# Last layer of a four-layer model: the two softplus functions with positive part and absolute value on ScalarE

## The reference, cut to what matters

```
dt = jax.nn.softplus(jnp.einsum('blr,dr->bld', time_step, dt_proj_w) + dt_proj_b)
delta = jax.nn.softplus(dt + dt_proj_b)
...
state = jnp.exp(d_t[..., None] * A) * state + (d_t * u_t)[..., None] * b_t[:, None, :]
```

## Time and profile before

| | |
|---|---|
| timed, median of 3 | 3816.14 us |
| profiled execution, its own time | 3796.93 us |
| span of the profiled execution | 3794.5 us |
| mean granted TensorE clock | 0.814 |
| TensorE matmul busy | 2954.5 us (78%) |
| VectorE busy | 2671.8 us (70%) |
| ScalarE busy | 1789.3 us (47%) |
| GpSimd busy | 448.2 us (12%) |

### The profile page before, as it was taken

One profiled execution on the slowest core, in us unless ns is written; L12 is line 12 of the kernel. 1 busy time (PEld: TensorE's weight loads), 2 busy tenths in 40 slices (PEclk: granted clock), 3 DMA queues, 4 the chain that ended last, 5 costly groups with the idle time before them and its releaser, 6 DMA issues. The chain is left out here.

```text
span 3794.5 us, 60184 instructions
## 1 busy us (share of the span) xinstructions
PE 2954.5 (78%) x19822; PEld 2399.8 (63%) x19822; DVE 2671.8 (70%) x7020; ACT 1789.3 (47%) x4073; POOL 448.2 (12%) x339
## 2 busy tenths in 40 slices
PE   3888888888989989899555567777777777777777
PEld 2666767767878878788444545555555555555555
DVE  3554554556666666666676279888888888888888
ACT  1222222225555555555334345555555555555555
POOL 0000000000000000000111312222211222222222
PEclk9887787788999999999667767677777777777777
DMA  5000000000000000000200211111111111111112
GB/s 163 0 0 0 0 0 0 0 0 1 0 0 0 0 0 0 0 0 0 65 8 15 58 53 46 46 45 35 45 46 45 46 45 46 45 45 41 40 45 67
DMA packets 66485, 103.57 MB, mean 27 GB/s; under 512 B 16808, under 2 KB 42032, under 8 KB 66352
## 3 DMA queue, kind: packets, MB, share of 16 engines
q1 hardware_dynamic: 63104, 97.36, 7.8%
q0 software_dynamic: 2048, 4.20, 0.4%
q10 hardware_dynamic: 1200, 0.27, 0.0%
HBM read 92.59 MB, written 9.21 MB: 27 GB/s over the span
## 5 line engine op out<-in xcount | busy, mean ns | idle before, releaser
L966 ACT ACTIVATE b_neg<-b_neg,b_nmax 128x128 f32<-128x128 f32 (+1 forms) x512 | 228.5, 447 | 272.9 <-DVE b_nmax L1074 271.6
L2229 POOL TENSOR_TENSOR d_state<-d_state 128x1024 f32<-128x1024 f32 x96 | 239.4, 2515 | 677.3 <-DVEq L2430 677.3
L2157 ACT ACTIVATE d_probs<-l_bank,w_b 128x256 f32<-128x256 f32 x512 | 210.8, 469 | 225.1 <-PE l_bank L2005 222.7
L2016 PE MATMUL l_bank<-w_w,d_probs 128*128 128x128 f32 x2048 | 267.7, 287 | 49.0 <-DVE same_head L2436 49.0
L2016 PEld LDWEIGHTS l_bank<-w_w,d_probs 128*128 128x128 f32 x2048 | 258.3, 201 | 64.5 <-issue 53.2
L2418 DVE TENSOR_TENSOR_SCAN d_state<-w,d_state 128x1024 f32<-128x1024 f32 x128 | 289.2, 2280 | 6.2 <-issue 6.2
L2005 PE MATMUL l_bank<-xnT,w_w 128*128 128x256 f32 x1024 | 248.1, 386 | 13.1 <-ACT d_probs L2157 13.1
L1062 DVE SCALAR_TENSOR_TENSOR b_gated<-b_th,l_bank 128x256 f32<-128x256 f32 x256 | 107.6, 420 | 207.9 <-ACT b_th L960 203.6
L607 ACT ACTIVATE a_hT<-l_bank,lnb,lnw 128x128 f32<-128x128 f32 x128 | 46.5, 468 | 423.9 <-PE l_bank L553 423.9
L518 PE MATMUL l_bank<-a_vmem,a_memT 128*128 128x128 f32 x768 | 185.2, 364 | 71.4 <-ACT a_h L602 71.4
L96 POOL TENSOR_TENSOR ln_rstd<-ln_var_eps,minus_half 128x2 f32<-128x2 f32 x51 | 35.3, 692 | 1670.5 <-DVE ln_var_eps L90 1670.5
(11 more groups left out here) (406 smaller groups left out, 7651.1 us busy)
## 6 DMA issues: line engine op xcount, KB each, us to landing
d_bct<-l_bc SPq DMA_DIRECT2D x132, 512.0 KB, 4.1
x_sorted<-x SPq DMA_DIRECT2D x1, 2176.0 KB, 15.2
w<-in_L_ffn_w_dram SPq DMA_DIRECT2D x1, 2048.0 KB, 10.1
w_w<-in_L_ffn_W_dram SPq DMA_DIRECT2D x1, 2048.0 KB
c2e_xg<-x_sorted SPq DMA_DIRECT2D x16, 128.0 KB, 2.3
y_sorted<-c2e_yo SPq DMA_DIRECT2D x16, 128.0 KB, 1.8
out_dram<-x SPq DMA_DIRECT2D x1, 2048.0 KB, 8.7
gating<-n_kernel_gating_EDF_dram SPq DMA_DIRECT2D x1, 1024.0 KB, 6.5
```

Of the source, the lines that this page charges most:

```text
L966: done = nc.scalar.activation(neg[:, h % RP, cols], neg[:, h % RP, cols], ACT.Exp, bias=nmax[:, h % RP, a:a + 1], scale=-1.0, accum_out=to ...
L2016: done = nc.tensor.matmul(bank[:, 4 + e % 2, a * D:(a + 1) * D], hid[:, e % 2, k, a * P:(a + 1) * P], w.w2[:, e, k, :], start=(k == 0), st ...
L2157: done = v.activation(hid[:, e % 2, k, :], bank[:, b, i * T:(i + 1) * T], ACT.Gelu, bias=w.b1[:, e, k:k + 1])
L2229: nc.gpsimd.tensor_tensor(st[i][:, 0:SG, :], st[i][:, 0:SG, :], st[i][:, SG * g:SG * (g + 1), :], ALU.add)
```

## The change

The argument work of both softplus functions moves from VectorE to ScalarE, and the second sum and `du` move from the end of a sequence to between the maxima of the second and the third score block of the next. `dneg_ready` is replaced by `half_ready`, which the first sum raises. `softplus_arg`, `first_part`, `second_part` and `third_part` go.

```
             def log_part(m, j):
-                act.wait_ge(dneg_ready, 2 * m + j + 1)
-                v.activation(dneg[:, :, :], dneg[:, :, :], ACT.Exp)
+                if j == 0:
+                    act.wait_ge(dt_in_psum, m + 1)
+                    act.wait_ge(rot_ready, m + 1)
+                    src = bank[:, 3, :].rearrange("p (i t) -> p i t", i=CI)
+                else:
+                    act.wait_ge(half_ready, m + 1)
+                    src = delta
+                for i in range(CI):
+                    v.activation(dv[:, i, :], src[:, i, :], ACT.Relu, bias=w.dt_b[:, i:i + 1])
+                for i in range(CI):
+                    done = v.activation(dneg[:, i, :], src[:, i, :], ACT.Abs, bias=w.dt_b[:, i:i + 1])
+                if j == 0:
+                    done.then_inc(dt_taken, 1)
+                v.drain()
+                v.activation(dneg[:, :, :], dneg[:, :, :], ACT.Exp, scale=-1.0)
                 v.drain()
                 v.activation(dneg[:, :, :], dneg[:, :, :], ACT.Ln, bias=1.0).then_inc(dlog_ready, 1)
...
             def softplus_sum(m, j):
                 dve.wait_ge(dlog_ready, 2 * m + j + 1)
-                done = v.scalar_tensor_tensor(out=delta[:, :, :], in0=dv[:, :, :], scalar=0.0, in1=dneg[:, :, :],
-                                              op0=ALU.max, op1=ALU.add)
-                if j == 1:
-                    done.then_inc(delta_ready, 1)
+                v.tensor_tensor(delta[:, :, :], dv[:, :, :], dneg[:, :, :], ALU.add)\
+                    .then_inc((half_ready, delta_ready)[j], 1)
+
+            def state_drive(m, par):
+                softplus_sum(m, 1)
                 v.drain()
                 v.tensor_tensor(du[:, :, :], delta[:, :, :], xs[:, par, :, :], ALU.mult)
...
-            first_part(0)
-            second_part(0)
-            third_part(0, 0)
+            softplus_sum(0, 0)
...
                         heads_max(blk)
                         if blk == 0:
                             norm_stats(nc, c, s, n + 1)
+                        if blk == 1:
+                            state_drive(n, par)
                     norm_rows(n + 1, 1 - par)
+                    v.drain()
...
                     add_expert(4)
-                    first_part(n + 1)
                     add_expert(5)
...
                     inner_stats()
-                    second_part(n + 1)
+                    softplus_sum(n + 1, 0)
                     inner_apply(rows[:, :, :], w.g2, w.be2, 2 * n + 2).then_inc(gate_ready, 1)
-                    third_part(n + 1, 1 - par)
```

More of the change, by code:

```diff
@@ L1853, in layer3 @@
         dt_taken = sem("dt_taken")
-        dneg_ready = sem("dneg_ready")
+        half_ready = sem("half_ready")
         dlog_ready = sem("dlog_ready")
```

## The result

Timed: 3872.5 us, the median of 4 runs (3866.2 to 3874.1), against 3814.0 us for the kernel before (4 runs). The ratio is 1.015, with a 95% interval of 1.0131 to 1.0169, so the change costs 50 to 64 us. The forecast was 3884 us, range 3845 to 3915, and slower.

A forecast was written before the change was run, and what follows sets the result against it. ScalarE was taken to set the time at the end of a sequence. 16 x (2.9 + 1.45) = 69.6, less 1.5, gave 68 us on the profiled 3796.93; with 19.2 us carried over, 3884 us, range 3845 to 3915.

The forecast's parts named there:

- First argument off VectorE: Before the last expert sum: 1.75 us of VectorE work goes but becomes idle, worth 0; bounds 0 and -1.75.
- Second argument off VectorE: Before the last layer norm: 1.30 us of VectorE work goes, but VectorE then waits for the Tanh; worth 0.
- First pass: Two Relu and two Abs on ScalarE behind the last Gelu: 1.70 us less 0.52 idle, making the copies 1.2 us late.
- Second pass: Relu and Abs on ScalarE behind the copies: 1.70 us, nothing hiding it; with the first pass, Tanh 2.9 us late.
- Second sum and `du` between the maxima: Moved from a wait for the Tanh into a VectorE block without idle: +1.45 us a sequence, bounds 0 and 1.5.
- Ahead of the loop: Second chain no longer waited for, but key copy and first scores later: -1.5 us once; bounds -5 and +1.7.
- The clock: TensorE's granted clock falls in some sequences before the last downs; from 20 us less to about as much more.
- VectorE's own work is the limit: Rival: Tanh ready when the second norm ends, 4.5 us a sequence saved, -72, 3744 us; chance 6%.
- Two more table loads: Rival: Relu or Abs need their own table ahead of Exp's, 1.28 us more each pass, +41, 3925 us; chance 7%.
- two fewer: Rival: Exp and Ln come from one table, the load before each Ln goes, -41, 3843 us; chance 7%.
- the hidden sum: Rival: the maxima wait for TensorE's scores, so the moved sum's 1.45 fills a gap, +45, 3861 us; chance 8%.
- signs of being wrong: VectorE idle before the gate under 3 us, sequence not over 3 us above 98.2, or added loads before Relu or Abs.

The follow-up runs named there:

- filled slot: Changed kernel with useless VectorE work, about 1.9 us, between the sums of experts 4 and 5, where the first argument had been: 3866.7 us, 1.0140.
- the move alone: Kernel before with only the second sum and `du` moved between the maxima, both arguments staying on VectorE: 3838.9 us, 1.0062.
- the changed kernel with the early sum: Changed kernel with VectorE's sum of expert 3 ahead of the first rotation instead of behind it: 3814.3 us, 0.9992.
- the last kernels: Changed kernel with Tanh ahead of the second softplus and sums of experts 3 and 4 early: 3725.1 us; the same with both arguments back on VectorE: 3767.5 us.
- the first two undoings: Changed kernel with one argument back on VectorE: the first argument, 3872.9 us, 1.0147; the second argument, 3861.1 us, 1.0117.
- exchanging two steps: Changed kernel with the gate's Tanh ahead of the second softplus on ScalarE instead of behind it: 3790.9 us, 0.9925.
- the last kernel: Kernel with Tanh ahead of the second softplus and sums of experts 3 and 4 early, with both arguments back on VectorE: 3767.5 us, 0.9885.

## Why the prediction was right

Right were the sign and the cause: ScalarE ends the sequence, and what is put ahead of its Tanh makes it longer. The range held the time; the forecast of 3884 us was 11.5 us too high.

- *First argument off VectorE, worth 0*: right. The filled slot shows it. The idle time came in two parts, in the sequence shown 0.68 us ahead of the last sum but one and 1.41 us ahead of the last, and not as 1.95 us in one.
- *Second argument off VectorE, worth 0*: right. With the argument back on VectorE the tail is shorter and not longer; what counts is ScalarE's pass.
- *First pass*: taken as 1.70, measured 1.53 (Gelu's end 3028.83 to the load at 3030.36), since the first Relu overlaps the Gelu. Less the slack I had it at 1.2 us; putting it back gave 0.87, because the first copy, which no longer waits for the turned heads, now also starts 0.10 us before the Ln ends.
- *Second pass*: taken as 1.70; putting it back gave 1.61. The late Tanh was 2.9 in the sum and 2.49 measured.
- *Second sum and `du` between the maxima*: taken as 1.45, measured 1.27 in the block of maxima, with the whole change and with the move alone.
- *Table loads*: none added, right.
- *Ahead of the loop*: -1.5 forecast. From the first Silu to the first maximum the trace has 15.11 us before (2209.16 to 2224.27) and 13.38 after (2221.84 to 2235.22): -1.73.
- *The clock*: the stretch from TensorE's release to the last sum grew from 9.23 to 9.48 us on the mean, 4 us in all, inside the 20 allowed.

The terms summed to 69.6 us where the two distances give 16 x 3.76 = 60. With 4 for the clock and 1.7 off ahead of the loop that makes 62.5 us, within the 50 to 64 of the timed interval. Mis-sized were the late Tanh (2.9 against 2.49) and the move (1.45 against 1.27), because I took the whole duration of a group and left out its overlap with its neighbours; that is 9.4 us of the 11.5. Another 2.1 us is the median of the kernel before, 3816.14 us when the forecast was made and 3814.0 with the fourth run. The clock's 4 us, which the forecast left at nothing, work the other way; as much again lies between the 62.5 us of the distances and the 58.5 of the medians, inside the interval. That these two cancel is luck. The step of 19.2 us from the profiled execution to the median did no harm, as it only puts the 68 us on the median; the profiled executions themselves can't be compared that way, since the changed kernel's lies on its median. Where the last layer begins differs that much from trace to trace with the same code ahead of it: the first maximum stands at 2224.3 us before, 2235.2 after, 2223.0 with the filled slot and 2253.4 in the changed kernel with the early sum.

Of the rivals, the one that VectorE's own work is the limit fell with the result; for the arguments it becomes true in the last kernels, where the waits are gone. Two more table loads and two fewer both fell with the five loads in the tail, and the hidden sum with the 1.27 us in the block of maxima, which the move alone has too.

Of the signs of being wrong none came. VectorE's idle before the gate is 6.19 us, and no load was added. The mean sequence is 101.52 us, 3.3 over the 98.2 that the prediction named. But that sign was set by too high a mean, from the window that is 1.57 us too wide; the two sequences of the stage table alone, 101.16 us each, would have missed it with 2.96, and against the true 97.5 they are 3.7 us longer. I did not see in the prediction that the move of the second sum made another order possible, in which the Tanh need not wait.

What stays open: the three lengths of TensorE's stretch went when its wait for the sum of expert 3 was cut, but what decides which of them a sequence gets is not shown. Nor is the time that the first two undoings lost ahead of the first expert sum explained by a run of its own. The traces say where it goes: the granted clock, low through the maxima, rises again about the start of attention's normalisation. Where it rises by 2.3 us after that start, the first expert sum comes 19.4 us after it, and where it rises later than 3 us, 19.7 to 20.3 us, in every sequence of all the traces. The second case has 2 of 15 sequences in the changed kernel, 5 with the first argument put back and 9 with the second.

## What to carry to other kernels

Ask of each instruction what stands behind it in its engine's queue. The activation that everyone waited for stood behind one that nobody needed yet; exchanging two steps brought 82 us, while the change that took work off the busiest engine had cost 58. And small steps are to be read from distances within the trace that one engine fixes; a TensorE that changes between its two clock levels swallowed 10 to 12 us by the distances of the trace in three of the runs here.

## What the runs showed of the hardware

- A Relu or an Abs of 128x256 with a bias pointer takes about as long as a Gelu: two from PSUM 0.84 to 0.86 us, two from SBUF 0.91.
- Neither needs a table load behind Gelu, Ln or Tanh. An Exp behind a Tanh needs none inside the loop body; at the head of the body, every second sequence, the decays have a load behind a Tanh all the same (8 in the changed kernel). An Exp behind an Ln has one, and an Ln behind an Exp, 1.28 us each time.
- TensorE's granted clock fell from 2.4 to 1.2 GHz about the end of a wait of 3.06 to 3.45 us in some sequences and not in others, and the stretch of 8.2 us behind it then took 9.5 to 11.2. With the wait cut to 1.36 us the stretch behind it had one length in all 16 sequences. In the last kernel the clock fell about 2 us behind a wait of 1.5 us in 7 of 15 sequences, so late that the last sum kept its place.
